# Score products of a head pair in two 64-row halves of the TensorE array, in place of one block-diagonal product

## What is computed

```python
x = x + attention(layernorm(x), ctx_1024, ctx_1024, Wq, Wk, Wv, Wo)
#   per pair of blocks (r, c) of a fixed list: softmax(q[r] @ k[c].T / 4, over the 64 keys of the block) @ v[c],
#   summed over c for each r; then @ Wo.T
x = x + ffn(layernorm(x))
#   gate: top 1 of 2 experts; masked x through w1/w2 of both experts, plus a shared expert,
#   each 256 -> 1024 -> 256 with relu
```

## Time and profile before

| what | value |
|---|---|
| median of 3 runs | 1029.49 us (1029.11 to 1031.79) |
| span of the profiled execution, first to last instruction | 1025.1 us |
| the profiled execution's own time | not listed; span and median differ by 4.4 us, which is what lies around the span, and the difference of two executions |
| TensorE matmul busy | 971.3 us (95%) |
| TensorE weight load busy | 848.3 us (83%) |
| VectorE, ScalarE, GpSimd busy | 655.2, 526.8, 464.9 us |
| mean granted TensorE clock | 0.972 of full speed |

### The profile page before, as it was taken

The page is one execution under the profiler, slowest core; times in us unless marked ns, Lnnn a source line. Parts: engine busy times, 40 slices in busy tenths (PEclk is TensorE's granted clock), DMA queues, the critical chain, the costliest instruction groups (busy, mean ns, idle before and its releaser), DMA issues.

```text
span 1025.1 us, 24123 instructions
## 1 busy us (share of the span) xinstructions
PE 971.3 (95%) x8864; PEld 848.3 (83%) x8864; DVE 655.2 (64%) x1074; ACT 526.8 (51%) x1197; POOL 464.9 (45%) x561
## 2 busy tenths in 40 slices
PE   3576999999999999999999999999999999999998
PEld 2346889798988979798897979889797988979788
DVE  4674566676666677566767766666776666676640
ACT  3253555546455555645555564545546454554544
POOL 7454436262443627244362724426272542726254
PEclk8586999999999999999999999999999999999999
DMA  9654261422626142262624226252422526240000
GB/s 247 159 128 75 62 85 46 69 48 61 92 61 82 57 62 44 65 89 61 82 65 56 43 71 82 61 82 72 51 44 73 78 61 86 68 57 20 17 12 11
DMA packets 72564, 71.40 MB, mean 70 GB/s; under 512 B 6224, under 2 KB 70352, under 8 KB 72544
## 3 DMA queue, kind: packets, MB, share of 16 engines
q1 hardware_dynamic: 70624, 64.83, 34.2%
q0 software_dynamic: 1920, 6.29, 2.2%
HBM read 48.03 MB, written 23.07 MB: 69 GB/s over the span
## 4 chain that ended last, share of the span: by engine, by line
PE 84%; DMA 7%; DVE 5%; POOL 1%; SPq 1%; issue 1%; ACT 1%; DVEq 0%; ACTq 0%; POOLq 0%
PE hid L349 26%; PE acc L491 25%; PE nd L416 12%; PE work L401 7%; PE work L386 5%; PE work L349 4%; DMA QP<-scratch_m 2%; PE work L444 2%; DMA scratch_m<-mT 2%; DVE xhat L717 2%; PE work L430 1%; DVE nmax L740 1%; DMA h<-w 1%; DMA QP<-scratch_q 1%; PE work L454 1%
## 5 line engine op out<-in xcount | busy, mean ns | idle before, releaser
L900 POOL TENSOR_TENSOR hl<-h,hh 128x256 fp32r<-128x256 f32 x384 | 284.8, 750 | 504.0 <-ACT hh L626 503.9
L626 ACT ACTIVATE h<-hid,bias 128x256 f32<-128x256 f32 x384 | 183.1, 477 | 295.8 <-PE hid L349 228.5
L746 DVE RECIPROCAL T<-nd 128x256 f32<-128x256 f32 x128 | 224.5, 1754 | 111.2 <-PE nd L416 111.2
L349 PE MATMUL hid<-X,w_hi 128*128 128x256 f32 x1536 | 289.1, 286 | 0.7 <-DVE X L697 0.7
L349 PEld LDWEIGHTS hid<-X,w_hi 128*128 128x128 f32 x1536 | 240.1, 189 | 26.8 <-issue 21.5
L349 PE MATMUL hid<-X,w_lo 128*128 128x256 f32 x768 | 216.3, 282 | 0.0
L491 PE MATMUL acc<-w_hi,hh 128*128 128x256 f32 x768 | 195.5, 288 | 0.0
L491 PE MATMUL acc<-w_lo,hh 128*128 128x256 f32 x768 | 189.1, 280 | 0.0
L740 DVE TENSOR_REDUCE nmax<-work 128x8 f32<-128x512 f32 x256 | 162.5, 682 | 39.2 <-PE work L386 38.3
L626 ACT ACTIVATE hh<-hid,bias 128x256 fp32r<-128x256 f32 x384 | 183.6, 478 | 0.0
L615 ACT ACTIVATE PT<-work 128x512 f32<-128x512 f32 x256 | 139.5, 604 | 67.9 <-PE work L401 67.9
(11 more groups left out here) (118 smaller groups left out, 1071.9 us busy)
## 6 DMA issues: line engine op xcount, KB each, us to landing
KP<-scratch_k SPq DMA_DIRECT2D x96, 128.0 KB, 4.9
QP<-scratch_q SPq DMA_DIRECT2D x96, 128.0 KB, 8.3
scratch_k<-T SPq DMA_DIRECT2D x16, 512.0 KB, 3.0
scratch_q<-T SPq DMA_DIRECT2D x16, 512.0 KB, 3.5
xin<-x SPq DMA_DIRECT2D x16, 256.0 KB, 9.6
ctx_in<-ctxT SPq DMA_DIRECT2D x16, 256.0 KB, 9.4
x<-x SPq DMA_DIRECT2D x16, 256.0 KB, 3.7
out<-x1b SPq DMA_DIRECT2D x16, 256.0 KB, 2.2
```

Source lines behind the costliest of these rows:

```text
L349: mm = nc.tensor.matmul(dst, R(s), R(m), start=n == 0, stop=n == len(steps) - 1)
L626: last = nc.scalar.activation(dst, hid[:, u % 2, a, :], ACT.Relu, bias=bias1[:, k:k + 1])
L746: nc.vector.reciprocal(T[:, p, :], nd[:, p % 2, 1, :]).then_inc(sem["inverted"], 1)
L900: nc.gpsimd.tensor_tensor(R(hl[:, u % 2, a]), h32[:, u % 2, a], hh[:, u % 2, a], ALU.subtract).then_inc(sem["hl_done"], 1)
```

## The change

Each head of a pair gets its own 64-row half: head 0 at rows 0 to 47, head 1 at rows 64 to 111, with its maxima and indicator (8 rows, `SROWS`) right behind, at rows 48 to 55 and 112 to 119. `KP` loses its second column set and its zeros. A scores call now covers one pair: four matmuls of 48 rows by 256 columns (2 token halves, 2 heads), a head's two in one bank. A transposed call covers a pair: four matmuls of 56 rows by 256 columns. A bank of scores is now one head with both token halves. `SCORE_STEPS` puts one pair before each of the first six FFN pieces and two before the seventh. Zeroing of `KP` and `QP` and VectorE's copy of the indicator go; in their place two DMAs read the indicator from `x1` into `KP`, and SyncE waits for them before it loads the residual into `x1`.

```diff
-SHIFT_ROW = 96
-SROWS = 16
-SCORE_STEPS = ((0,), (1, 2, 3), (4, 5, 6), (7, 8), (9, 10), (11, 12, 13), (14, 15))
+KROWS = 3 * HD
+SROWS = 2 * NBLK
+SCORE_STEPS = ((0,), (1,), (2,), (3,), (4,), (5,), (6, 7))
-        QP, KP = sb("QP", [P, PAIRS, SEQ]), sb("KP", [P, PAIRS, 2, SEQ])
+        QP, KP = sb("QP", [P, PAIRS, SEQ]), sb("KP", [P, PAIRS, SEQ])
...
-                        r = 48 * s + 16 * slot
-                        sp.dma_start(KP[r:r + HD, :, s, :], src[s]).then_inc(sem["k_spread"], 16)
+                        r = 64 * s + 16 * slot
+                        sp.dma_start(KP[r:r + HD, :, :], src[s]).then_inc(sem["k_spread"], 16)
...
-                for part in range(2):
-                    r = SHIFT_ROW + 8 * part
-                    sp.dma_start(QP[r:r + 8, :, :], scratch_m[part].rearrange("(p r) t -> r p t", r=8)) \
+                for s in range(2):
+                    r = 64 * s + KROWS
+                    sp.dma_start(QP[r:r + SROWS, :, :],
+                                 scratch_m.rearrange("(p s b) x t -> s (b x) p t", s=2, b=NBLK)[s]) \
...
-            sp.wait_ge(sem["zeroed"], 6)
             spread(16, "first_q_bounced", "first_k_bounced")
+            sp.wait_ge(sem["indicator_loaded"], 16)
+            for s in range(2):
+                r = 64 * s + KROWS
+                sp.dma_start(KP[r:r + SROWS, :, :], x1[0:SROWS, 0, None, :].to_broadcast([SROWS, PAIRS, SEQ])) \
+                    .then_inc(sem["indicator_placed"], 16)
+            sp.wait_ge(sem["indicator_placed"], 32)
...
-            def scores(i, j):
-                bank = claim(i, ("s", j))
+            def scores(i, p):
+                banks = [claim(i, ("s", 2 * p))]
...
-                nc.tensor.matmul(bank, R(QP[0:SHIFT_ROW, p, P * t:P * t + P]), R(KP[0:SHIFT_ROW, p, :, :]),
-                                 start=True, stop=True).then_inc(sem["s_full"], 1)
+                for t in range(TT):
+                    for s in range(2):
+                        if t == 0 and s == 1:
+                            banks.append(claim(i, ("s", 2 * p + 1)))
+                        r = 64 * s
+                        mm = nc.tensor.matmul(banks[s][:, SEQ * t:SEQ * t + SEQ],
+                                              R(QP[r:r + KROWS, p, P * t:P * t + P]),
+                                              R(KP[r:r + KROWS, p, :]), start=True, stop=True)
+                        if t == TT - 1:
+                            mm.then_inc(sem["s_full"], 1)
...
-                p, s = j // 2, j % 2
                 for t in range(TT):
-                    mm = nc.tensor.matmul(bank[:, SEQ * t:SEQ * t + SEQ], R(KP[:, p, s, P * t:P * t + P]),
-                                          R(QP[:, p, :]), start=True, stop=True)
-                mm.then_inc(sem["st_full"], 1)
+                    for s in range(2):
+                        if t == 0 and s == 1:
+                            banks.append(claim(i, ("st", 2 * p + 1), more))
+                        r = 64 * s
+                        mm = nc.tensor.matmul(banks[s][:, SEQ * t:SEQ * t + SEQ],
+                                              R(KP[r:r + KROWS + SROWS, p, P * t:P * t + P]),
+                                              R(QP[r:r + KROWS + SROWS, p, :]), start=True, stop=True)
+                        if t == TT - 1:
+                            mm.then_inc(sem["st_full"], 1)
...
-                nc.vector.tensor_reduce(nmax[:, t, 8 * p:8 * p + 8],
-                                        work[:, BANK[("s", j)], :].rearrange("q (b k) -> q b k", k=BLOCK),
+                nc.vector.tensor_reduce(nmax[:, :, NBLK * j:NBLK * j + NBLK],
+                                        work[:, BANK[("s", j)], :].rearrange("q (t b k) -> q t b k", t=TT, k=BLOCK),
...
-            rows = slice(SHIFT_ROW, SHIFT_ROW + SROWS)
-            for s in range(2):
-                nc.vector.tensor_copy(R(KP[rows, :, s, :]), x1[rows, s, None, :].to_broadcast([SROWS, PAIRS, SEQ]))
...
-            nc.gpsimd.memset(KP[:, :, :, :], 0.0).then_inc(sem["zeroed"], 1)
...
-            nc.gpsimd.memset(QP[:, :, :], 0.0).then_inc(sem["zeroed"], 1)
```

More of the change, by code:

```diff
@@ L47 @@
 QSCALE = HD ** -0.5
-SHIFT_ROW = 96
-SROWS = 16
-SCORE_STEPS = ((0,), (1, 2, 3), (4, 5, 6), (7, 8), (9, 10), (11, 12, 13), (14, 15))
+KROWS = 3 * HD
+SROWS = 2 * NBLK
+SCORE_STEPS = ((0,), (1,), (2,), (3,), (4,), (5,), (6, 7))
 PAIR_UP = {0: 6, 3: 7, 6: 8}
 PAIR_DOWN = {1: 5, 4: 6, 7: 7}
-S_JOBS = [("s", j) for j in range(PAIRS * TT)]
+S_JOBS = [("s", j) for j in range(HEADS)]
 ST_JOBS = [("st", j) for j in range(HEADS)]
@@ L66 @@
 EVACUATED = {
-    "s": ("max_done", PAIRS * TT), "mT": ("m_lo", 1),
+    "s": ("max_done", HEADS), "mT": ("m_lo", 1),
     "xT": ("xT_lo", 1), "k": ("k_lo", 1), "q": ("q_lo", 1), "v": ("v_copied", 1),
@@ L83 @@
 SEMS = (
-    "ident_loaded indicator_loaded consts_loaded proj_loaded0 proj_loaded1 proj_loaded2 proj_loaded3 "
+    "ident_loaded indicator_loaded indicator_placed consts_loaded proj_loaded0 proj_loaded1 proj_loaded2 proj_loaded3 "
     "stage_loaded0 stage_loaded1 stage_loaded2 stage_loaded3 stage_loaded4 stage_loaded5 stage_loaded6 "
@@ L160, in xattn_ffn @@
         scratch_k = nc.dram_tensor("scratch_k", [2, D, SEQ], F32, kind="Internal").ap()
-        scratch_m = nc.dram_tensor("scratch_m", [2, HEADS * NBLK, SEQ], F32, kind="Internal").ap()
+        scratch_m = nc.dram_tensor("scratch_m", [HEADS * NBLK, 2, SEQ], F32, kind="Internal").ap()
         def w1_piece(w, n):
@@ L261, in shift @@
                 for t in range(TT):
-                    sp.dma_start(scratch_m[:, :, P * t:P * t + P].rearrange("h r q -> r h q"),
+                    sp.dma_start(scratch_m[:, :, P * t:P * t + P],
                                  mT[rows * t:rows * t + rows, :, :]).then_inc(sem["m_bounced"], 16)
                 sp.wait_ge(sem["m_bounced"], 32 * n + 32)
-                for part in range(2):
-                    r = SHIFT_ROW + 8 * part
-                    sp.dma_start(QP[r:r + 8, :, :], scratch_m[part].rearrange("(p r) t -> r p t", r=8)) \
+                for s in range(2):
+                    r = 64 * s + KROWS
+                    sp.dma_start(QP[r:r + SROWS, :, :],
+                                 scratch_m.rearrange("(p s b) x t -> s (b x) p t", s=2, b=NBLK)[s]) \
                         .then_inc(sem["shift_spread"], 16)
@@ L301, in _ @@
             load_projection(3)
-            sp.dma_start(x1[SHIFT_ROW:SHIFT_ROW + SROWS, :, :], indicator).then_inc(sem["indicator_loaded"], 16)
+            sp.dma_start(x1[0:SROWS, 0, :], indicator).then_inc(sem["indicator_loaded"], 16)
             for dst, src in ((bias1[:, :], b1), (bsum[:, :], blocksum), (hsum[:, :, :], headsum),
@@ L378, in front_v @@
                 mm.then_inc(sem["v_full"], 1)
-            def scores(i, j):
-                bank = claim(i, ("s", j))
-                if j == 0:
+            def scores(i, p):
+                banks = [claim(i, ("s", 2 * p))]
+                if p == 0:
                     pe.wait_ge(sem["q_spread"], 96 * i + 96)
                     pe.wait_ge(sem["k_spread"], 96 * i + 96)
-                t, p = j // PAIRS, j % PAIRS
-                nc.tensor.matmul(bank, R(QP[0:SHIFT_ROW, p, P * t:P * t + P]), R(KP[0:SHIFT_ROW, p, :, :]),
-                                 start=True, stop=True).then_inc(sem["s_full"], 1)
+                for t in range(TT):
[8 more added lines that the diff above has]
+                            mm.then_inc(sem["s_full"], 1)
@@ L389, in maxima, with scores_t @@
             def maxima(i):
                 bank = claim(i, ("mT", 0))
-                pe.wait_ge(sem["max_done"], PAIRS * TT * (i + 1))
+                pe.wait_ge(sem["max_done"], HEADS * (i + 1))
                 nc.tensor.transpose(bank[:, 0:P], nmax[:, :, :].rearrange("q t r -> q (t r)"), id32[:, :]) \
                     .then_inc(sem["mT_full"], 1)
-            def scores_t(i, j, more):
-                bank = claim(i, ("st", j), more)
-                if j == 0:
+            def scores_t(i, p, more):
+                banks = [claim(i, ("st", 2 * p), more)]
+                if p == 0:
@@ L506, in iteration @@
                 for step, jobs in enumerate(SCORE_STEPS):
-                    for j in jobs:
-                        scores(i, j)
+                    for p in jobs:
+                        scores(i, p)
                     if step % 2 == 0:
@@ L525, in iteration @@
                 scores_t(i, 0, more)
-                scores_t(i, 1, more)
                 for p in range(PAIRS):
@@ L532, in iteration @@
                     if p + 1 < PAIRS:
-                        scores_t(i, 2 * p + 2, more)
-                        scores_t(i, 2 * p + 3, more)
+                        scores_t(i, p + 1, more)
                     values(i, p)
@@ L680, in _ @@
             projection_high(3)
-            act.wait_ge(sem["zeroed"], 6)
+            act.wait_ge(sem["zeroed"], 4)
             front_v(0, acc[:, :, :])
@@ L737, in maximum @@
```

(24 more changed lines are left out.)

## The result

The changed kernel takes 1045.36 us (median of 4, 1044.67 to 1046.83) against 1030.45 before: 1.5% slower, ratio 1.0148 with a 95% interval of 1.0128 to 1.0168. The forecast was 1057, plus 27.5; measured is plus 14.9.

What follows compares the result with a forecast made beforehand. TensorE, open for 95% of the span, was taken to bound the kernel. 15 x (2.0 scores - 0.4 transposed scores) + 3.5 start = plus 27.5 us, forecast 1057 us; range 994 to 1075, the forecast's own 1041 to 1075.

Steps and rivals of the forecast that it cites:

- the rival of 1048: Halves run one after the other and switching is free; stall and `maxima` cost 1.0 us per iteration; chance 0.07.
- a round of two halves: Scores and transposed scores: two 64-row matmuls of 256 columns run at once, taking 0.118 us.
- switching, a visit between whole-array work: Entering and leaving 64-row work costs a drain and an exposed weight load each way, 0.42 us in all.
- last step and `maxima`: Last scores step: TensorE waits for pair 6's maximum, plus 0.91 us, and plus 0.06 at `maxima`.
- scores in all: Scores stage per iteration: streaming -1.88, switching +2.94, last step +0.91, `maxima` +0.06, in all plus 2.0 us.
- `maxima`'s way back: From `maxima` to the first transposed scores: work, chain and the wait there stay as they are, change 0.
- transposed scores: Transposed scores stage per iteration: streaming -1.88, switching +1.47, in all minus 0.4 us.
- sum: Change per iteration, scores plus transposed scores: plus 1.6 us, taken 15 times.
- The start: Program start: later residual and ctx cost 2.5 us, the first iteration's scores 1, in all plus 3.5 us.
- Free switching: Rival: switching costs nothing and halves run together, -2.0 us per iteration, 1003 us; chance 0.31.
- half price: Rival: switching costs half, 2.2 us less per iteration than forecast, 1024 us; chance 0.11.
- No overlap: Rival: halves don't run together and switching is dear, plus 5.4 us per iteration, 1114 us; chance 0.13.

Runs made afterwards that it cites:

- products twice: The changed kernel with each score product issued twice, 8 matmuls per pair instead of 4: 1071.98 us.
- whole-array run: Against the kernel with only the scores in halves: same order, banks and steps, but each score product over 112 rows of the whole array; 1041.11 us.
- control pair: Kernel before with only the new row layout and one extra transfer, 1028.83 us, against that with transposed scores in halves too, 1018.94 us.
- layout run: The kernel before with only heads at rows 0 and 64 and one extra transfer, all products over the whole array: 1028.83 us, ratio 0.9989.

## Why the prediction was right, and where it was off

Direction and mechanism came out as put: halves do run together, and switching and the new order eat more than that brings. The size was nearly twice what was measured, and the total alone would rather have spoken for the rival of 1048; it is the parts that tell them apart. Term by term, per iteration:

| term | predicted | measured | from |
|---|---|---|---|
| a round of two halves | 0.118 | 0.12 | products twice |
| switching, a visit between whole-array work | 0.42 | 0.38 to 0.41 | step of 2.04; whole-array run |
| last step and `maxima` | 0.97 | 0.93 | whole-array run |
| scores in all | +2.0 | +1.9 | 15.48 - 13.75, and 0.18 ahead |
| `maxima`'s way back | 0 | -0.24 | 7.96 to 7.72 |
| transposed scores | -0.4 | -0.76 | 24.88 to 24.12 |
| sum | +1.6 | +0.9 | 60.4 - 59.5 |

*The way back* is the step that failed. I wrote that the chain behind `maxima` stays as it is and so does its wait. It had a term that depends on when it runs: VectorE's normalization beside GpSimd's addition. Delayed by the scores, it met less of that addition, and in the changed kernel none. In the run with the new order and nothing else this gave back 0.26 + 0.11 of 0.93.

*Transposed scores* were mis-sized. Of the 0.76 in the table, 0.11 is the way back's again. In the control pair they are worth (832.98 - 822.89) / 14 = 0.72 per iteration (from the first score of iteration 1 to that of iteration 15). Five calls gain 0.05 each in place of 0.02, two 0.24 as predicted, and pair 0, which I charged with a full way in and out less its streaming, plus 0.19, pays next to nothing: before, it waited for the transfer and its load was exposed (0.74 for four matmuls in the chain, where 0.47 is streaming), so the way in was paid already. The load ahead of a wait is as little hidden as the load ahead of a switch.

*The start* came to 4.0 in the profiles (2.7 to the first score, 1.3 in the first iteration) for a predicted 3.5, but this agreement is worth nothing. Of the 2.7, the kernel before with only its steps changed shows 1.9, and the layout run shows 3.8 and a median that is no longer than before. By the medians, 15 x 0.9 = 13.5 of the 14.9 us are the iterations, which leaves some 1.4 for the start and all else.

*One term was missing.* In the last iteration of the profiled execution the granted clock fell to its lower level for a while; the stretch here covers it:

```profile
970.00:980.00 10.00, 9.44 (x77) 5.43 (x79) 6.55 (x6) 4.97 (x12) 1.45 (x2) 0.66 0.00 0
```

TensorE had waited for ScalarE's exponentials just before, as it does in the kernel before, where the clock stayed up. The stage took 25.7 us, against 22.7 in the same kernel with the order of halves or the start changed, where the clock stayed up too; 3 us of the profile's span. With only the transposed scores in halves the clock fell there too, for a shorter time (24.2 us), so this doesn't come in every profile; how often it comes isn't known.

*The rivals.* Free switching, 1003 us, fell with the 0.19 that every FFN piece behind a visit takes longer, and half price, 1024, with the 0.38 of a whole visit. No overlap, 1114, fell with the doubled products. So did the rival that came nearest in number, no gain and no switch, 1048: a round of two halves costs 0.12 and not 0.24, and the scores stage took 15.5 us where that rival gives 14.7. Of the Trainium skill's page "TensorEngine Tiling (Array Packing)", section "Key Properties", the rule that a change of tiling mode drains TensorE agrees with these runs (0.38 to 0.41 a visit, with a weight load exposed at each end), and so does its sentence that tiles load weights and multiply in parallel.

## What to carry to other kernels

Two row halves double the pace, but going to them from whole-array matmuls and back costs what some three rounds of 256 columns save (0.38 against 0.118 a round): a visit of two rounds loses, as did seven here, and by these figures one of four would just win, which no run here compares. Where a switch is paid anyway, next to 32-column work or behind a wait, halves are nearly free, and applying them to the transposed scores alone gave 1018.9 us, 1.1% better than before. And a ring of three banks that was deep enough for the old steps stalls when two pairs, four banks' worth, come in one step: look which evacuation each claim waits for before you change the grain.

## What the runs showed that I had not expected

The order of instructions between two halves doesn't matter: with (half 0, half 0, half 1, half 1) the third load started 7 ns after the first and the second 0.109 after it. And scores stages made slower by 0.61 and 0.93 us cost only 0.2 and 0.6 in the iteration (59.5 before, 59.75 with steps alone, 60.1 with the whole-array run), since the first of VectorE's two normalizing instructions shrank from 1.48 to 0.72 and 0.46 us as it came to lie later against GpSimd's addition.
